# Moving the moving operands of a mixture-of-experts stage 32 bytes further in SBUF

## The reference: what is computed

```python
x = x + layernorm(attention(layernorm(x)))        # one head of width 256, softmax over 1024 keys
x = x + layernorm(ffn(layernorm(x)))

def ffn(h):                                       # h: 8192 tokens x 256
    scores = softmax(h @ gate_w.T).T              # 16 experts x 8192 tokens
    topk_weight, topk_idx = top_k(scores, 1024)   # each expert takes its 1024 best tokens
    xg = h[topk_idx]
    g, u = xg @ Wg.T, xg @ Wu.T                   # 256 -> 1024
    eo = (gelu(g) * u) @ Wd.T * topk_weight       # 1024 -> 256
    out = zeros.at[topk_idx].add(eo)
    shared = (gelu(h @ Sg.T) * (h @ Su.T)) @ Sd.T # 256 -> 512 -> 256, for all tokens
    return out + shared
```

## The kernel before

| tensors | first byte | mod 64 | mod 256 |
|---|---|---|---|
| `wg1`, `wu1`, `wg0`, `wu0` (hi, lo), `wd` | 38016 to 103552 | 0 | 128 |
| `XG1`, `OUT` and in it `wp` | 119936, 136832 | 0 | 128 |
| attention: `xnT`, `tT`, `V`, `Pr`, `PT` | 151968 to 219552 | 32 | 160 |
| attention: `wv`, `m` | 143456 to 149856 | 32 | 96 or 224 |
| moe: `XT0`, `XT1`, `HF`, `H`, `XG0` | 142848 to 204288 | 0 | 0 |
| moe: `halves` (`XTF` lies over it), `turned`, `val` | 213152 to 221728 | 32 | 160 or 32 |

## Time and profile before

### The profile page before, as it was taken

How to read it: one execution, slowest core, us unless ns; L and a number is a source line. 1 busy time by engine, 2 the same in 40 slices (tenths; PEclk the granted TensorE clock), 3 DMA queues, 4 the chain that set the end, 5 groups by cost and what they waited for, 6 DMA issues and landing times.

```text
span 1975.7 us, 29127 instructions
## 1 busy us (share of the span) xinstructions
PE 1948.8 (99%) x10638; PEld 1657.2 (84%) x10638; DVE 1366.5 (69%) x2602; ACT 1036.0 (52%) x1929; POOL 523.8 (27%) x626
## 2 busy tenths in 40 slices
PE   7999999999999999999999999999999999999997
PEld 6888888888888888888888888888888888888886
DVE  6777787777776778667676766656565656565647
ACT  4457576666655434445444544545454545445455
POOL 0031132123120001222432333243234323332246
PEclk9999999999999999999999999999999999999999
DMA  3103323333243111434434443443435344434566
GB/s 129 54 33 108 76 98 108 97 100 114 66 162 130 65 65 47 130 79 103 87 87 102 93 98 77 108 87 96 96 89 106 86 105 92 101 83 99 157 214 171
DMA packets 153338, 197.38 MB, mean 100 GB/s; under 512 B 104448, under 2 KB 121088, under 8 KB 145152
## 3 DMA queue, kind: packets, MB, share of 16 engines
q1 hardware_dynamic: 127824, 158.00, 25.6%
q0 software_dynamic: 25392, 37.77, 12.1%
HBM read 114.38 MB, written 59.34 MB: 88 GB/s over the span
## 4 chain that ended last, share of the span: by engine, by line
PE 67%; DVE 2%; POOL 1%; issue 1%; ACT 0%; DVEq 0%; ACTq 0%; POOLq 0%
PE mo_psD L1626 12%; PE mo_psG L60 7%; PE mo_psU L60 7%; PE mo_psU L62 7%; PE mo_psG L62 7%; PE mo_psG L61 7%; PE mo_psU L61 7%; PE mo_psD L1628 6%; PE mo_psD L60 1%; PE mo_psD L62 1%; PE mo_psD L61 1%; PE mo_psX L1351 1%; DVE mo_F L1940 1%; POOL mo_H_lo L2279 0%; POOL mo_rs L2289 0%
## 5 line engine op out<-in xcount | busy, mean ns | idle before, releaser
L1755 ACT ACTIVATE mo_HF<-mo_psG 128x512 f32<-128x512 f32 x320 | 191.3, 598 | 401.6 <-PE mo_psU L62 375.1
L2261 POOL DMA_INDIRECT ACC<-OUT,mo_GI x128 | 201.7, 1576 | 642.0 <-DVE OUT L2050 630.4
L1967 DVE TENSOR_TENSOR mo_HF<-mo_psU,mo_HF 128x512 f32<-128x512 f32 x320 | 220.4, 689 | 210.7 <-ACT mo_HF L1755 206.5
L1626 PE MATMUL mo_psD<-wd,mo_H_hi 128*128 128x512 f32 x1024 | 360.8, 393 | 0.2 <-DVE OUT L2050 0.2
L1628 PE MATMUL mo_psD<-wd,mo_H_lo 128*128 128x256 f32 x1024 | 289.3, 283 | 0.0
L60 PE MATMUL mo_psG<-mo_XT_hi,wg_hi 128*128 128x512 f32 x640 | 255.5, 399 | 0.4 <-DVE mo_HF L1967 0.4
L60 PE MATMUL mo_psU<-mo_XT_hi,wu_hi 128*128 128x512 f32 x640 | 253.5, 396 | 0.0
L62 PE MATMUL mo_psU<-mo_XT_hi,wu_lo 128*128 128x512 f32 x640 | 252.7, 395 | 0.0
L62 PE MATMUL mo_psG<-mo_XT_hi,wg_lo 128*128 128x512 f32 x640 | 252.6, 395 | 0.0
L61 PE MATMUL mo_psG<-mo_XT_lo,wg_hi 128*128 128x512 f32 x640 | 252.4, 394 | 0.0
L61 PE MATMUL mo_psU<-mo_XT_lo,wu_hi 128*128 128x512 f32 x640 | 252.4, 394 | 0.0
(11 more groups left out here) (354 smaller groups left out, 4154.6 us busy)
## 6 DMA issues: line engine op xcount, KB each, us to landing
X1a<-wg_in SPq DMA_DIRECT2D x16, 1024.0 KB, 5.2
X1a<-wu_in SPq DMA_DIRECT2D x16, 1024.0 KB, 4.8
X1a<-wd_in SPq DMA_DIRECT2D x16, 1024.0 KB, 4.8
XN<-XG SPq DMA_DIRECT2D x8, 1088.0 KB, 4.2
X<-x_in SPq DMA_DIRECT2D x8, 1024.0 KB, 5.4
out_dram<-X SPq DMA_DIRECT2D x8, 1024.0 KB, 6.4
XN2T<-xn2T SPq DMA_DIRECT2D x8, 1024.0 KB, 5.1
X1a<-xt_in SPq DMA_DIRECT2D x7, 1024.0 KB
```

The costliest lines, as they stand in the source:

```text
L1626: pe.matmul(psD[:, t % 2, :], h_hi, wd_both[:, it, :, :].rearrange("p z d -> p (z d)"), start=(it == 0), stop=False)
L1755: a.activation(HF[:, it % 2, :], psG[:, it % 2, :], ACT.Gelu).then_inc(s_gelu, 1)
L1967: v.tensor_tensor(HF[:, it % 2, :], psU[:, it % 2, :], HF[:, it % 2, :], ALU.mult).then_inc(s_mul, 1)
L2261: g.indirect_dma_start(out=io["ACC"], out_offset=bass.IndirectOffsetOnAxis(ap=GI[n % 2][:, 4 * tb + t:4 * tb + t + 1], axis=0), in_=OUT[:, ...
```

## The change

One tensor of 8 float32 numbers (32 bytes in each partition), which nothing reads or writes, is allocated ahead of `XT`:

```diff
         wd = [wd_both[:, :, z, :] for z in (0, 1)]
+        new("lead", [P, 8])
         XT = [pair(f"XT{i}", [P, KD, 512]) for i in range(2)]
         HF = new("HF", [P, 2, 512])
         H = pair("H", [P, NI + 2, 512])
```

## The result

Nine runs of the changed kernel have a median of 1982.75 us, nine of the kernel before 1977.57 us: a ratio of 1.0025, 95% interval 1.0016 to 1.0033. The kernel became slower by 5.2 us, 0.26%, which is just clear of no change.

A forecast was written before the change was run, and what follows sets the result against it. It took TensorE's matmul pace as the bound, the other engines having room. Matmuls, other engines and DMAs each counted zero, so the sum was 0 against 1975.7 us profiled, 1977 us against the median; 8-in-10 range 1955 to 1993 us.

The forecast's parts named there:

- What bounds the kernel: Whole kernel: TensorE is busy 99% of 1975.7 us, so time is the number of matmuls times their pace.
- TensorE's waits under 1 us: Sign in moe that no change is right, beside up steps at 2.78 to 2.79 us and down pairs at 0.351.
- Attention must stay: Sign in attention: matmuls stay at 230 ns (scores) and 347 ns (V pairs); otherwise the difference is not the change's.
- VectorE, ScalarE, GpSimd and the DMAs at nothing: Other engines' accesses and the gathers and transposes: moved offsets cost zero time, any small loss being hidden behind TensorE.
- The matmuls at zero: Up, expert down and shared down matmuls: changed operand offsets cost 0, between bounds of 13.8 us off and 78 us more.
- no change: Whole kernel: likeliest case, 1977 us, own range 1974 to 1981 us, chance 0.40.
- The first reason: Projection of the last sequences: both operands at 0 modulo 64, yet 116.5 ns a matmul, as fast as attention.
- The second reason: Up steps in moe: operands lie at quite different addresses, yet both steps take the same 2.79 and 2.78 us.
- The third: Third reason for zero: matmul durations in the groups hardly tell attention and moe apart, 393 ns against 394.
- The collision: Up and down matmuls: stationary load and moving stream meet more often at mixed alignment; 19.5 us slower, 1997 us, chance 0.23.
- Attention's pace: Up and down matmuls: low address bits set the pace, now as in attention; 13.8 us faster, 1963 us, chance 0.37.
- The two rules: Trainium skill: gather rows 32 bytes further cost one beat more, unseen; independent read ports make the matmul change worth zero.

The follow-up runs named there:

- `e1_xt32`: Against the kernel before, only the XT tensors stand 32 bytes further, the others at their old places modulo 256; 1984.83 against 1979.71 us, ratio 1.0024.
- `e3_all32`: Against the kernel before, everything in SBUF stands 32 bytes further, so distances between operands stay; 1979.57 against 1979.71 us, ratio 0.9998.
- `e4_micro`: The kernel's computation left out, TensorE alone runs 84 matmuls per setting of operand offsets; 512 columns take 228.0 to 235.2 ns at 32-byte steps.

## Why the prediction was wrong

*What bounds the kernel.* Right: TensorE is busy 99% before and after, none of its waits grew, and the time is the number of matmuls times their pace. Two details were wrong. The 0.4 and 0.2 us were not all of TensorE's waits in moe: 2.1 us for `mo_F` and 2.2 for its own sequencer stand there too, before and after, so "TensorE's waits under 1 us" could not have come true. And the profiled execution of 1975.7 us does not go with the time of 1975.69: each run with both figures on record has a time 1.8 to 2.1 us above its span, so this one took about 1977.5 us, the median. The forecast of 1977 us stays the same by that.

*Attention must stay.* Right: without the intervals above 300 ns, the mean over all its score matmuls is 229.3 or 229.4 ns in every version, and over its V pairs 348 ns.

*VectorE, ScalarE, GpSimd and the DMAs at nothing.* Right: 685 ns against 686, the gather into `mo_XG` lands after 2.8 us against 2.9, and `e1_xt32` has the whole loss with the other tensors at their old places modulo 256. The extra beats of the gathers, if there are any, are not seen in the time.

*The matmuls at zero.* This is the step that failed: "I take zero, for three reasons." Its measured value is +6.9 us by the intervals and +5.2 in the medians, which is outside the 1974 to 1981 us that I gave to no change and inside the range of 8 in 10. The first reason compared places modulo 64 (the projection, both operands at 0, as fast as attention), but `e3_all32` and the stationary offsets 0, 128 and 160 of `e4_micro` show that the place does not count and the distance does. In the projection the distances change from matmul to matmul (0, 64, 128 and 192, as the rows of `wp` are 1088 bytes long). The second reason took operands at quite different addresses as evidence, but all of these are multiples of 512 bytes apart, so the low bits never varied. The third compared durations of groups, 393 against 394 ns, whose ends are modelled; the intervals of the same rows, 230.0 against 232.1, said more, and I had worked them out.

*The rivals.* The collision (0.23) had the right sign, and two up steps at 2.81 us came close to its 2.82. Its price of 19.5 us was nearly four times too high; it put the loss into every up and down matmul, where the experts' down pairs got 0.7 ns faster; over its 6656 matmuls 5.2 us are 0.8 ns each, under the 1 ns that it named. Its mechanism is not borne out in the form I gave it: narrower weight loads do not lower the surplus in proportion. Attention's pace (0.37) was wrong for 32 bytes, yet it saw that low address bits set the pace. That its 13.8 us are close to what 128 bytes bring, 1976.89 - 1963.33 = 13.6, is luck: there the up matmuls win 4.9 ns each, not 2.1, and the pairs lose 2.0 instead of winning 4.2. The signal was read rightly and put down to the wrong quantity, the place in place of the distance. A look at both columns of my own table of places (moe: 0 and 128 modulo 256, attention: 160 and 160) would have offered it.

*The two rules.* The Trainium skill, TensorE: Matmul & The Clock Gate, sections "Part 2: What happens when you issue a matmul" and "Back-to-back issue gap", gives two independent read ports and, for an isolated matmul of 512 columns, 215.8 ns. The trace of TensorE alone disagrees with the figure: 226.7 ns, once running, is the fastest of all settings with a weight load for each matmul, and by the distance and finer offsets the pace changes by up to 11 ns. Whether the two reads meet at the ports or elsewhere, no run shows. The Trainium skill, SBUF — State Buffer, section "Specifications (TRN2)", has 16-byte lines and a penalty for each cross to a new one. A start inside a line could explain the 239 ns at 4 bytes off, but 8 bytes off, inside a line too, it is 234.5, and with both operands 16 bytes off, at the start of a line, 234.1 ns; these do not follow from it.

*What stays open.* Why the distance acts at all, and modulo what beyond 256 (moving whole tensors by 256 changed nothing in the pairs of `e1_xt32`), is not settled. Nor is what part the width of the load has, which of the two stationary operands counts, or what picks the rhythm where two are possible.

## What to carry to other kernels

Where TensorE is busy all the time, take the intervals from start to start of the same form of matmul in two stages and compare them; a difference of 1% with no waits is worth looking into, and here it was worth 19 us. Before such tensors are laid out, run the matmul form alone over a few distances between moving and stationary operand in steps of 32 bytes, 84 matmuls each, leave the first intervals out, and then choose the padding for each form; the best distance is not the same for each. Run each setting more than once and with something else ahead of it, as one setting can have two rhythms. In a blind forecast, ask of every "it has no effect" whether the rows that show it have varied the quantity at all.

## What the runs showed of the hardware

Float32 hi/lo matmuls of 512 columns, with a 128-column weight load for each, run on TensorE at 228.0 to 235.2 ns by the distance of their operands, in steps of 32 bytes, and at 239.1 ns with 4 bytes off, at the 2.4 GHz level (mean granted clock 0.997); once running, at 226.7 to 234.3 ns. Their intervals form a fixed rhythm, for instance of seven, which returns in another kernel at the same distance. The surplus over the 213.3 ns of the columns is 13 to 26 ns. With a stationary operand of 32 columns in place of 128 it is 17 to 20 ns, more than with 128 columns at distance 0 and less at 128 and 160. VectorE's two-input operation of 512 columns takes 684 to 686 ns with its operands at 0 or 32 modulo 64.
